# How the split queries of an attention layer reach their stacked layout: 32 small copies from SBUF, or two stores to DRAM and eight loads

## Chip, cores and metric

The kernel runs on one NeuronCore of a Trainium2 chip. The metric is the device time of one execution in microseconds; the figure given is the median of several executions.

## What is computed

Two transformer-like layers over x of shape (8, 512, 128), with AdaLN modulation (a scale, a shift and a gate per batch element). The program handles one batch element (512 tokens) at a time:

```python
# layer 0
h = layernorm(x) * (1 + ca) + sa
x = x + ga * attention(h)          # 8 heads, 2 KV groups, keys and values through a latent of 32, causal softmax
h = layernorm(x) * (1 + cb) + sb
x = x + gb * moe(h)                # 8 experts of 64, top 2, gelu
# layer 1
h = layernorm(x) * (1 + ca) + sa
x = x + ga * selective_scan_mixer(h)   # 256 channels, 16 states, 512 steps
h = layernorm(x) * (1 + cb) + sb
x = x + gb * moe(h)                # 8 experts of 512, top 2, gelu

# the mixer's recurrence, for each of 16 states n
dA  = exp(delta * A[n]);  dBx = (delta * xc) * Bm[n]
h_t = dA_t * h_(t-1) + dBx_t;  y += h_t * Cm[n]
```

The attention's scores need the queries to nearly full f32 precision. Because keys come from a latent of width 32, the key projection is folded into the queries, so that a head's scores are a product over 32 latent rows only. The kernel fills the 128 rows of the array with four such blocks: both queries and keys are split into a high part and a rest, and the four products of the parts are stacked. For the queries the four blocks of rows are high, rest, high, rest (`TERMS = 4`).

## The kernel before, in words

**Engines and order.** Each engine has its own instruction stream written out by hand; semaphores (`signal`, with a target computed per batch) join them. `B = 8` batches are software-pipelined: while batch b goes through the mixer's scan, TensorE and ScalarE do the large experts of batch b-1 in pieces (`SCAN_HIDDEN`, `SCAN_OUTPUT`, `SCAN_GELU` and `SCAN_ADD` say after which step of the scan which piece comes), and the queries, keys and values of batch b+1 are projected in the middle of batch b.

**Queries.** ScalarE copies the projected queries to `q_lat` (two groups g of 128 rows, which are 4 heads j of 32 latent rows, by 512 tokens). VectorE (`split_heads`, L1182) writes the high part `q_hi` and signals `q_split`; GpSimd (`split_rest`, L500) writes the rest `q_lo` and signals `q_rest`. Both lie in the tile `probs`. In `q_terms` all 8 heads must lie on the same 32 partitions, one block of 32 partitions per term. So a head's rows change partitions, and SyncE does this by DMA: `place_queries` (L379 to L390) sends, for each half, group and head, two copies of 32 partitions by 512 floats (64 KB each, 2 KB a partition), 32 in all, each issued at L389. They signal `q_placed`. TensorE's first score product of a batch (`scores(0)`, L717 and L725) waits for all of them, and so does VectorE once in the scan (L1519), since the products that it writes from then on overwrite `probs`.

**The scan.** Before a scan, ScalarE writes the projection `proj` (L1087, signals `pr_out`) and later `dt_log` (L1096, signals `dt_l`). VectorE makes delta (L1499) and u = delta * xc (L1503, once per half c of the channels). SyncE's `spread_rows` (L405 to L418) stores the 16 rows of B to DRAM (L408), waits for that, and loads them back in 8 pairs p, each broadcast to all 128 partitions (L417, 512 KB), into a ring of three slots; pair 1 waits for `dt_l`, and from pair 3 on each waits until GpSimd has used the slot. For each state n and half c, ScalarE computes the decay (L1102) into a ring of three PSUM banks, GpSimd computes the injected term u * B[n] (L455 for state 0, one instruction per half; L457 for the others, both halves at once), VectorE runs the recurrence (`tensor_tensor_scan`, L1514, 32 instructions a batch) and multiplies by C[n], which TensorE has broadcast (L896), into `probs` (L1192); GpSimd (L473, L476) and TensorE (L686) add the 16 products up. After the first three decays ScalarE loads the Gelu table, does four Gelus of the experts of batch b-1 and loads the table for exponentials again (`SCAN_GELU[2]`, L1108, L957, L1111); batch 0 has no experts behind it and no such detour.

**SyncE's order.** SyncE issues the weights, then `place_queries(0)`, then the rows of gates. After that, for each batch b from 0 to 6, `place_queries(b + 1)` and then `spread_rows(b)`, one after the other in one queue; the last batch has `spread_rows(7)` only.

The scan of batch b is called scan b here; there are eight.

## Time and profile before

| | |
|---|---|
| median of 3 runs | 1392.23 us (1390.68 to 1392.95) |
| the profiled execution, its own time | 1388.01 us |
| its span, first to last instruction | 1386.2 us |
| mean granted TensorE clock | 0.942 |
| busy, share of the span: TensorE, VectorE, ScalarE, GpSimd | 82%, 75%, 61%, 38% |
| q_terms<-probs, 256 issues of 64 KB | 2.0 us each from issue to landing |
| probs_T<-b_rows_dram (rows of B), 64 issues of 512 KB | 3.7 us |
| share of 16 DMA engines used by the hardware queue q1 | 13.1% |

The tile `probs_T` shares its space with the scan's tiles (the rows of B, the injected terms and the states), and `step_space` holds delta and u, so the rows of the trace show these names. Row names drop buffer numbers. The engines' names in the rows are PE (TensorE matmul), PEld (its weight load), DVE (VectorE), ACT (ScalarE), POOL (GpSimd) and SP (SyncE); a name with a q is the engine's queue, which issues DMAs.

### The profile page before, as it was taken

The numbers are of one execution on the slowest core, as the hardware profiler recorded it, in microseconds if no ns is written. First come the engines' busy times: TensorE is split into PE (matmuls) and PEld (weight loads), VectorE is DVE, ScalarE is ACT, GpSimd is POOL, SyncE is SP. The second block draws the span as 40 slices with busy tenths as digits, with TensorE's granted clock in tenths as the row PEclk, the third lists the DMA queues.
The fourth block names the chain that finished last, engine by engine and source line by source line (L and its number), as shares of the span: only waits on it lengthen the run. The fifth ranks groups of instructions, "written<-read, shape, count | busy, mean of one in ns | idle before, by whom it ended". The sixth has DMA issues, their size and how long they took to land. (4 is left out here: it accounts for less than half of the span.)

```text
span 1386.2 us, 19199 instructions
## 1 busy us (share of the span) xinstructions
PE 1137.4 (82%) x6304; PEld 727.3 (52%) x6304; DVE 1041.9 (75%) x2396; ACT 847.5 (61%) x1600; POOL 531.9 (38%) x325
## 2 busy tenths in 40 slices
PE   3684678989788887989789887988889897898698
PEld 2551135546555455555656456655556465555456
DVE  2476987589866998579876898669975898669822
ACT  1444346579556866478655876468664785469342
POOL 1003950268102960249202870049402680029400
PEclk8796579999999999999999999999999999999899
DMA  7203200131003200131002300041001300011000
GB/s 262 96 1 108 76 8 1 41 113 31 16 1 105 79 2 15 25 113 46 17 1 62 107 16 17 3 121 61 16 1 43 113 29 9 1 62 62 8 0 9
DMA packets 27731, 65.80 MB, mean 47 GB/s; under 512 B 8048, under 2 KB 8936, under 8 KB 27248
## 3 DMA queue, kind: packets, MB, share of 16 engines
q1 hardware_dynamic: 25328, 56.00, 13.1%
q0 software_dynamic: 1296, 4.20, 1.0%
q10 hardware_dynamic: 1008, 4.38, 0.8%
q8 instruction: 51, 0.84, 0.3%
q14 instruction: 48, 0.39, 0.1%
HBM read 45.40 MB, written 2.38 MB: 34 GB/s over the span
## 5 line engine op out<-in xcount | busy, mean ns | idle before, releaser
L1514 DVE TENSOR_TENSOR_SCAN probs_T<-bank,probs_T 128x512 f32<-128x512 f32 x256 | 303.3, 1210 | 34.6 <-POOL probs_T L455 29.5
L641 PEld LDWEIGHTS bank<-w_w,hidden 128*128 128x128 f32 x2048 | 247.8, 192 | 80.7 <-issue 76.9
L625 PE MATMUL bank<-hT,w_w 128*128 128x512 f32 x512 | 265.6, 636 | 27.2 <-ACT hidden L957 26.3
L457 POOL TENSOR_TENSOR probs_T<-step_space,probs_T 128x1024 f32<-128x1024 f32 x120 | 282.0, 2359 | 1.8 <-DVE probs_T L1514 1.8
L641 PE MATMUL bank<-w_w,hidden 128*128 128x128 f32 x2048 | 251.7, 276 | 9.4 <-DVE expert_sum L1204 9.0
L957 ACT ACTIVATE hidden<-bank,w_b 128x512 f32<-128x512 f32 x256 | 169.6, 686 | 122.2 <-PE bank L625 121.6
L1030 ACT ACTIVATE probs<-bank,row_neg 128x128 f32<-128x128 f32 (+3 forms) x256 | 135.0, 530 | 149.8 <-DVE row_neg L1365 134.7
L1102 ACT ACTIVATE bank<-step_space,a_neg 128x512 f32<-128x512 f32 x256 | 168.6, 684 | 67.8 <-DVE probs_T L1514 49.5
L625 PEld LDWEIGHTS bank<-hT,w_w 128*128 128x128 f32 x512 | 90.9, 198 | 156.1 <-ACT hidden L957 97.9
L1365 DVE TENSOR_REDUCE row_neg<-bank 128x1 f32<-128x128 f32 (+3 forms) x256 | 120.3, 483 | 68.4 <-PE bank L727 66.2
L476 POOL TENSOR_TENSOR step_space<-step_space,probs 128x512 f32<-128x512 f32 x112 | 142.1, 1269 | 61.3 <-DVE probs L1192 61.2
L735 PE MATMUL bank<-w_ident,probs 128*128 128x128 f32 x640 | 117.9, 284 | 48.5 <-ACT probs_T L1006 24.3
L1192 DVE TENSOR_TENSOR probs<-probs_T,bank 128x1024 f32<-128x1024 f32 x128 | 153.1, 1196 | 2.3 <-POOL step_space L473 2.0
L686 PE MATMUL bank<-probs,w_ident 128*128 128x512 f32 x256 | 145.1, 650 | 10.3 <-DVE probs L1192 10.3
L725 PE MATMUL bank<-k_terms,q_terms 128*128 128x128 f32 (+3 forms) x256 | 104.9, 426 | 21.8 <-DMA q_terms<-probs 21.8
L1204 DVE SCALAR_TENSOR_TENSOR expert_sum<-bank,gates,expert_sum 128x128 f32<-128x128 f32 x256 | 71.3, 340 | 56.9 <-PE bank L641 55.3
L482 POOL TENSOR_TENSOR gated_out<-w_out_w,gate 128x256 f32<-128x256 f32 x8 | 5.7, 719 | 270.7 <-DVE xn L1244 270.7
L735 PEld LDWEIGHTS bank<-w_ident,probs 128*128 128x128 f32 x640 | 70.2, 143 | 63.9 <-ACT probs L1030 36.9
L896 PE MATMUL bank<-split,select 96*128 96x512 bf16 x128 | 52.6, 411 | 53.6 <-DVE probs L1192 50.9
L455 POOL TENSOR_TENSOR probs_T<-step_space,probs_T 128x512 f32<-128x512 f32 x16 | 20.3, 1287 | 177.6 <-DMA probs_T<-b_rows_dram 137.3
L1006 ACT ACTIVATE probs_T<-bank 128x128 f32<-128x128 f32 (+3 forms) x176 | 74.8, 425 | 16.0 <-PE bank L735 16.0
L482 POOL TENSOR_TENSOR gated_proj<-w_wprojT,gate 128x512 f32<-128x512 f32 x8 | 17.6, 2203 | 126.8 <-DVE xn L1244 126.8
(186 smaller groups left out, 1682.0 us busy)
## 6 DMA issues: line engine op xcount, KB each, us to landing
probs_T<-b_rows_dram SPq DMA_DIRECT2D x64, 512.0 KB, 3.7
q_terms<-probs SPq DMA_DIRECT2D x256, 64.0 KB, 2.0
w_w<-in_w_dram ACTq DMA_DIRECT2D x2, 2048.0 KB, 13.9
x_in<-in_x_dram POOLq DMA_DIRECT2D x8, 256.0 KB, 3.4
gate<-gate_rows_dram SPq DMA_DIRECT2D x1, 2048.0 KB, 7.2
out_dram<-x_out POOLq DMA_DIRECT2D x7, 256.0 KB, 2.8
step_space<-in_wmod_dram SPq DMA_DIRECT2D x1, 768.0 KB, 5.5
probs_T<-in_wqT_dram SPq DMA_DIRECT2D x1, 512.0 KB, 3.9
```

Of the source, the lines that this page charges most:

```text
L457: ins = nc.gpsimd.tensor_tensor(inject[:, n % 3, :, :], u[:], row.unsqueeze(1).to_broadcast([P, DH, T]), ALU.mult)
L476: ins = nc.gpsimd.tensor_tensor(state_sum[:, 1, :], state_sum[:, 1, :], read[:, n % 2, 1, :], ALU.add)
L625: mm(hid1_bank(n)[:], w["w1"][:, n // C1, n % C1 * P:(n % C1 + 1) * P], hT[3][:], start=True, stop=True).then_inc(hid1_mm.sem, 1)
L641: ins = mm(to[:, t * P:(t + 1) * P], hidden[:, (e * C1 + c) % (2 * C1), t * P:(t + 1) * P], w["w2"][:, e * C1 + c, :], start=(c == 0), sto ...
L686: mm(bank[SUM_BANK][:], ident[:], read[:, n % 2, 0, :], start=(n == 0), stop=(n == NS - 1)).then_inc(sum_mm.sem, 1)
L735: ins = tr(bank[4 + n % 2][:, k * P:(k + 1) * P], probs_ring[:, n % 4, k * P:(k + 1) * P], ident[:])
L957: f(hidden[:, n % (2 * C1), :], hid1_bank(n)[:], ACT.Gelu, bias=w["b1"][:, n:n + 1]).then_inc(hid1_act.sem, 1)
L1030: f(probs_ring[:, n % 4, 0:(i + 1) * P], bank[SCORE_BANK[n % 4]][:, 0:(i + 1) * P], ACT.Exp, bias=row_neg[:, n % 4:n % 4 + 1], accum_out=r ...
L1102: f(decay(k)[:], delta[:, c, :], ACT.Exp, scale=a_neg[:, c, n:n + 1]).then_inc(dec_ok.sem, 1)
L1192: tt(read[:, n % 2, :, :], state[:, n % 2, :, :], bank[C_BANK][:].unsqueeze(1).to_broadcast([P, DH, T]), ALU.mult).then_inc(rd_ok.sem, 1)
L1365: v.reduce_max(row_neg[:, n % 4:n % 4 + 1], bank[SCORE_BANK[n % 4]][:, 0:(i + 1) * P], AX_X, negate=True).then_inc(s_max.sem, 1)
L1514: v.tensor_tensor_scan(state[:, n % 2, c, :], decay(DH * n + c)[:], inject[:, n % 3, c, :], 0.0, ALU.mult, ALU.add).then_inc(st_ok.sem, 1)
```

## The change

The queries' two parts are each stored whole to a DRAM tensor in one transfer of 256 KB (`save_queries`), and each of the four blocks of `q_terms` is then loaded from there in two transfers of 256 KB, one per group, whose source is read in the order row, head, token (`place_queries(b, r)`). For the first batch this happens in one go. For the others the stores stand where the 32 copies stood, and the loads of block r are issued in the scan of the batch before, right behind the rows of B of pair r + 2. VectorE's wait in the scan (L1519) is now for the two stores, TensorE's is for eight loads.

```diff
--- before.py
+++ after.py
@@ -220,6 +220,7 @@
             return bank[DECAY_BANK[k % 3]]
 
 
+        q_dram = nc.dram_tensor("q_parts_dram", (2, P, G * T), F32)
         b_dram = nc.dram_tensor("b_rows_dram", (NS, T), F32)
 
         weights_in, experts_in = sem("weights_in"), sem("experts_in")
@@ -259,7 +260,8 @@
         k_split = signal("k_split", 1)
         q_rest = signal("q_rest", 1)
         k_rest = signal("k_rest", 1)
-        q_placed = signal("q_placed", 16 * TERMS * H)
+        q_saved = signal("q_saved", 32)
+        q_placed = signal("q_placed", 16 * TERMS * G)
         v_mm = signal("v_mm", 1)
         v_out = signal("v_out", 1)
         UNITS = G * NT * HG
@@ -376,18 +378,20 @@
 
         @block.sync
         def _(sp):
-            def place_queries(b):
-
-                for half, source in enumerate((q_hi, q_lo)):
-                    if half == 0:
-                        sp.wait_ge(q_split.sem, q_split.at(b, 1))
-                    else:
-                        sp.wait_ge(q_rest.sem, q_rest.at(b, 1))
-                    for g in range(G):
-                        for j in range(HG):
-                            for r in range(half, TERMS, 2):
-                                sp.dma_start(q_terms[r * L:(r + 1) * L, g * HG + j, :].bitcast(F32), source[j * L:(j + 1) * L, g, :]
-                                             ).then_inc(q_placed.sem, 16)
+            def save_queries(b):
+
+                for half, (signal_of, source) in enumerate(((q_split, q_hi), (q_rest, q_lo))):
+                    sp.wait_ge(signal_of.sem, signal_of.at(b, 1))
+                    sp.dma_start(q_dram[half, :, :], source.rearrange("p g t -> p (g t)")).then_inc(q_saved.sem, 16)
+
+            def place_queries(b, r):
+
+                if r == 0:
+                    sp.wait_ge(q_saved.sem, q_saved.at(b, 32))
+                for g in range(G):
+                    rows = q_dram[r % 2, :, g * T:(g + 1) * T].rearrange("(j l) t -> l j t", l=L)
+                    sp.dma_start(q_terms[r * L:(r + 1) * L, g * HG:(g + 1) * HG, :].bitcast(F32), rows
+                                 ).then_inc(q_placed.sem, 16)
 
             for name in first_a:
                 sp.dma_start(w[name][:], io[name]).then_inc(first_in, 16)
@@ -395,7 +399,9 @@
                 sp.sem_inc(s.sem, 1)
             for name in then:
                 sp.dma_start(w[name][:], io[name]).then_inc(weights_in, 16)
-            place_queries(0)
+            save_queries(0)
+            for r in range(TERMS):
+                place_queries(0, r)
             sp.wait_ge(setup_gate, 4)
             sp.dma_start(gates_dram[:, :], gate_rows[:].rearrange("p k d -> p (k d)")).then_inc(gates_saved, 16)
             sp.wait_ge(gates_saved, 16)
@@ -416,9 +422,11 @@
                         sp.wait_ge(inj_p.sem, inj_p.at(b, 2 * (p - 3) + 3))
                     sp.dma_start(b_wide[:, slot, :, :], rows[:, 2 * p:2 * p + 2, :].to_broadcast([P, 2, T])
                                  ).then_inc(b_rows[p % 3].sem, 16)
+                    if b < B - 1 and 2 <= p < 2 + TERMS:
+                        place_queries(b + 1, p - 2)
 
             for b in range(0, B - 1):
-                place_queries(b + 1)
+                save_queries(b + 1)
                 spread_rows(b)
             spread_rows(B - 1)
 
@@ -714,7 +722,7 @@
                 def scores(n):
                     g, i, j = n // (NT * HG), n // HG % NT, n % HG
                     if n == 0:
-                        pe.wait_ge(q_placed.sem, q_placed.at(b, 16 * TERMS * H))
+                        pe.wait_ge(q_placed.sem, q_placed.at(b, 16 * TERMS * G))
                         pe.wait_ge(k_rest.sem, k_rest.at(b, 1))
                         pe.wait_ge(v_out.sem, v_out.at(b, 1))
                         if ending:
@@ -1516,7 +1524,7 @@
                         if c == 0 and n >= 1:
                             read_product(b, n - 1)
                     if n == 0 and b < B - 1:
-                        dve.wait_ge(q_placed.sem, q_placed.at(b + 1, 16 * TERMS * H))
+                        dve.wait_ge(q_saved.sem, q_saved.at(b + 1, 32))
                     if n in SCAN_ADD:
                         early(EARLY_E + SCAN_ADD.index(n))
                 check()
```

## Rows read from the trace of the kernel before

**Rows 1.** The page, section 1: busy time, share of the span and instructions of each engine.

```profile
PE 1137.4 (82%) x6304; PEld 727.3 (52%) x6304; DVE 1041.9 (75%) x2396; ACT 847.5 (61%) x1600; POOL 531.9 (38%) x325
```

**Rows 2.** Waits, whole run: waiting engine, line, releaser: total us, times, longest.

```profile
POOL probs_T L455 <- DMA probs_T<-b_rows_dram: 137.3, 7, 20.2
...
DVE probs_T L1514 <- POOL probs_T L455: 29.5, 8, 4.9
```

**Rows 3.** Timeline of SyncE: start us, length us, line, operation, count.

```profile
22.20 20.22 SPq L389 DMA_DIRECT2D q_terms<-probs  x32
...
579.96 21.80 SPq L389 DMA_DIRECT2D q_terms<-probs  x32
601.80 0.58 SPq L408 DMA_DIRECT2D b_rows_dram<-proj  x1
```

**Rows 4.** Timeline of all engines around the start of scan 3; idle time before in brackets.

```profile
581.74 2.36 POOL L500 TENSOR_TENSOR probs<-q_lat,probs 128x1024 fp32r<-128x1024 f32 x1
...
594.98 0.69 ACT L1087 ACTIVATE proj<-bank,w_x_proj_b 112x512 f32<-112x512 f32 x1 [0.16 <-PE bank L867]
...
602.47 1.91 ACT L1102 ACTIVATE bank<-step_space,a_neg 128x512 f32<-128x512 f32 x3 [1.96 <-DVE step_space L1499]
...
608.94 2.42 DVE L1514 TENSOR_TENSOR_SCAN probs_T<-bank,probs_T 128x512 f32<-128x512 f32 x2 [4.88 <-POOL probs_T L455]
...
612.07 1.30 ACT L1102 ACTIVATE bank<-step_space,a_neg 128x512 f32<-128x512 f32 x2
```

**Rows 5.** Timeline of ScalarE and VectorE in scan 7.

```profile
1237.21 1.91 ACT L1102 ACTIVATE bank<-step_space,a_neg 128x512 f32<-128x512 f32 x3 [1.96 <-DVE step_space L1499]
...
1246.88 2.67 ACT L1102 ACTIVATE bank<-step_space,a_neg 128x512 f32<-128x512 f32 x4
...
1247.60 2.34 DVE L1514 TENSOR_TENSOR_SCAN probs_T<-bank,probs_T 128x512 f32<-128x512 f32 x2 [2.65 <-ACT bank L1102]
...
1299.42 1.21 DVE L1514 TENSOR_TENSOR_SCAN probs_T<-bank,probs_T 128x512 f32<-128x512 f32 x1
```

**Rows 6.** Timeline: first decays and last scan instruction of scan 1, then scan 6.

```profile
284.93 1.91 ACT L1102 ACTIVATE bank<-step_space,a_neg 128x512 f32<-128x512 f32 x3 [1.96 <-DVE step_space L1499]
...
348.89 1.22 DVE L1514 TENSOR_TENSOR_SCAN probs_T<-bank,probs_T 128x512 f32<-128x512 f32 x1
...
1080.17 1.91 ACT L1102 ACTIVATE bank<-step_space,a_neg 128x512 f32<-128x512 f32 x3 [1.96 <-DVE step_space L1499]
...
1144.61 1.21 DVE L1514 TENSOR_TENSOR_SCAN probs_T<-bank,probs_T 128x512 f32<-128x512 f32 x1
```

**Rows 7.** Timeline of GpSimd and VectorE at the start of scan 0.

```profile
135.07 2.48 POOL L455 TENSOR_TENSOR probs_T<-step_space,probs_T 128x512 f32<-128x512 f32 x2 [18.53 <-DMA probs_T<-b_rows_dram]
...
136.46 2.41 DVE L1514 TENSOR_TENSOR_SCAN probs_T<-bank,probs_T 128x512 f32<-128x512 f32 x2 [2.32 <-POOL probs_T L455]
```

**Rows 8.** Timeline; landing of L389, 22 to 26 us; page; windows (PEclk, DMA share, GB/s last).

```profile
21.07 2.34 POOL L500 TENSOR_TENSOR probs<-q_lat,probs 128x1024 fp32r<-128x1024 f32 x1 [18.89 <-DVE probs L1182]
...
43.96 0.45 PE L725 MATMUL bank<-k_terms,q_terms 128*128 128x128 f32 x1 [21.78 <-DMA q_terms<-probs]
...
DMA to landing us min/median/max: 2.0/2.3/3.3
...
probs_T<-b_rows_dram SPq DMA_DIRECT2D x64, 512.0 KB, 3.7
...
out_dram<-x_out POOLq DMA_DIRECT2D x7, 256.0 KB, 2.8
...
26.00:42.00 16.00, 0.00 (x0) 0.00 (x0) 0.00 (x0) 0.00 (x0) 0.38 (x1) 0.50 0.43 105
...
607.00:609.00 2.00, 2.00 (x3) 0.68 (x2) 0.06 (x1) 0.45 (x1) 1.45 (x2) 0.50 1.01 387
```

**Rows 9.** Timeline of scan 3: a load of rows of B, and GpSimd's first use.

```profile
612.36 0.32 SPq L417 DMA_DIRECT2D probs_T<-b_rows_dram  x1
...
624.00 2.36 POOL L457 TENSOR_TENSOR probs_T<-step_space,probs_T 128x1024 f32<-128x1024 f32 x1
```

## The prediction

> **What bounds the kernel now.** I read the page first: TensorE is busy 82% of the span, no engine all of it [rows 1], so the question is which engine ends each stage. The waits of the whole run came next. Two rows concern the queries' copies. GpSimd's first product of a scan (L455) waited 137.3 us for rows of B from DRAM, seven times, and VectorE's first scan (L1514) waited 29.5 us for that product [rows 2]. There are eight scans, and the one without the DMA wait is the last, the only one with no next queries to place. SyncE's timeline gives the reason [rows 3]. In batch 3 its 32 placements (L389) keep it issuing from 579.96 for 21.80 us, 0.68 us each, and right behind them, at 601.80, comes the store of B (L408). But the projection that this stores was written from 594.98 to 595.67 [rows 4]: the store stood 6.1 us behind placements. At the start the same 32 issues run from 22.20 to 42.42 while TensorE waits 21.78 us for the queries, until 43.96 [rows 3, 8].
>
> Inside a scan VectorE is the engine that ends last; its instructions follow each other without gaps, so what its early part gains moves the end of the stage. Which wait comes next is read from scans 3 and 7, side by side [rows 4, 5].
>
> **The change, part by part.** It removes 32 issues before B, adds 2 stores (256 KB each) there, and 8 loads (256 KB each) behind rows of B. The bytes placed stay 2 MB a batch, plus 0.5 MB stored. The sum has three terms.
>
> *Scans 1 to 6.* SyncE takes the two stores, an issue of 0.58 us each as L408's [rows 3]. In batch 3 the low part that the second waits for is there at 584.10 [rows 4], so SyncE is free some 10 us before the projection is written. So the rows of B come some 6 us earlier and the wait of L455 on the DMA goes. Next late are VectorE's own inputs, then ScalarE. VectorE's idle time there is 4.88 us in scan 3 [rows 4], and this is not what is won: ScalarE, after three decays, leaves for four Gelus and two table loads (SCAN_GELU[2]) and is back at 612.07, 9.60 us after its first decay at 602.47, with nothing of it dependent on B [rows 4]. The decay for the fourth scan instruction cannot be earlier. Scan 7 shows how that looks when B is not late: decay at 1237.21, ScalarE back at 1246.88, the instruction at 1247.60 after 2.65 us idle for ScalarE [rows 5]. So scan 7 is my template. From first decay to last scan instruction it takes 1299.42 - 1237.21 = 62.21 us [rows 5]; scans 1 to 6 take 63.96, 63.49, 64.47, 64.14, 64.12 and 64.44 (the first and the last of the six in [rows 6]). The excesses over 62.21 add up to 11.4 us, which I take; the bounds are nothing (rival 3) and all of VectorE's idle (rival 2).
>
> *Scan 0.* No experts run, so ScalarE has no detour. VectorE idles 2.32 us from 134.14, when the second half of u is made. GpSimd's second product, 1.24 us, then ends near 135.4 instead of 137.55 [rows 7], and the third scan instruction waits for the product after it. Gain 2.1 us.
>
> *The start.* Nothing hides it: TensorE stands still until the queries are placed. The high parts are stored at 22.20 as now; the low ones exist when GpSimd ends at 23.41 [rows 8]. The nearest store of 256 KB (out_dram) lands in 2.8 us [rows 8]; it is on GpSimd's queue, but the low store would land at 23.45 + 2.8 = 26.3. A queue still full of weights costs up to 1.3 us (the first placements landed in 3.3 instead of 2.0 [rows 8]), all of it before the high store, which has that time. Then 8 loads. Issuing them, at 0.58 us, is 4.6 us; what ends last is their transfer. The old placements moved 105 GB/s at a DMA share of 0.43 [rows 8], so a full share onto 32 partitions would be 105 / 0.43 = 244 GB/s, 1.07 us for 256 KB, 8.6 us for eight. With 1.7 us from issue to landing besides the bytes (2.0 less 0.27), the last lands at 26.3 + 1.7 + 8.6 = 36.6: gain 43.96 - 36.6 = 7.4 us. Bounds: at the rate of B's rows onto 128 partitions (387 GB/s over 2 us at full share [rows 8]) each takes 0.68 us and the gain is 10.5; at the old pace, 105 GB/s, each takes 2.5 us and the start loses 4.0. I take 1.07, since same destination, same 2 KB pieces are its nearest row, and as the old pace was set by SyncE's issue, with the engines less than half busy. Whatever follows in batch 0 (gate rows, weights) waits on work that moves with it.
>
> The Trainium skill's page "SBUF — State Buffer", section on the DMA port swizzle, says that 32 partitions reach only half the ports, some 218 GB/s; by that, an estimate, the eight take 9.6 us and the start gains 6.3. Its page "DMA: Bandwidth & Descriptors" (anatomy of one DMA) speaks against a detour over DRAM, since a completion there waits for the slowest receipt, about 2 us; the 2.8 us store in the row already carries that.
>
> *Costed at nothing.* The 8 loads of a scan: behind the rows for pairs 2 to 5 SyncE only waits for GpSimd. In scan 3 the fourth rows were issued at 612.36 and first used at 624.00 [rows 9]; landing takes 3.7 [rows 8], so 7.9 us are spare and two loads take 2.1. If that cover were gone, GpSimd and with it the scan would wait; the rival below prices that. The first three rows of B go ahead of any load. The loads need the stores landed, and those were issued before B. The last pair stands behind rows 5 of 8, with almost half of the 62 us of a scan left before the first user, L725. VectorE's wait at L1519, now for two stores instead of 32 placements, cost no idle time before and none now. Q_terms is free: its last reader was the attention before. TensorE's c_mm waits are for VectorE's products and move with them.
>
> Sum: 7.4 + 2.1 + 11.4 = 20.9 us. The profiled execution took 1388.0 us (span 1386.2), so 1367.1 for it; the median shown is 1392.2, 4.2 us or 0.3% above, and the forecast for a median is 1392.2 - 20.9 = 1371.3.
>
> **Rivals.**
> 1. *The loads at the start keep the old pace* (2.5 us each, DRAM reading no better than 105 GB/s). Start -4.0, scans +13.5: 9.5 us, 1382.7. For: small pieces, few partitions; against: the DMA share of 0.43. Chance 0.10.
> 2. *ScalarE does not hold the scan*, all of VectorE's idle goes: 29.5 less scan 0's 2.3 [rows 2, 7], and less 0.2 that scan 7 waited with B in time, is 27.0 in place of 11.4, total 36.5, 1355.7. Against: scan 7. Chance 0.05.
> 3. *The scans' gain is given back*, TensorE or GpSimd being the one that ends the scan: 7.4 + 2.1 only, 1382.7. Against: scan 7 carries the same expert pieces without a gap. Chance 0.06.
> 4. *SyncE is not freed*, B still waiting behind the low store: only the start counts, 1384.8. The low part was made 11 us before the projection [rows 4]. Chance 0.01.
> 5. *Slower: the loads are slow and hold the queue.* If one takes T us, the start gains 43.96 - 28.0 - 8T, and in seven scans four pairs each stand before rows of B that have 7.9 us to spare. The start alone eats all 13.5 us of the scans at T = 3.7; beyond 3.95 each pair adds 2T - 7.9, 28 times. At T = 4.1 the start loses 16.8 and the pairs 8.4: 11.7 us slower, 1403.9. For it: both kinds share one queue. Against: 64 GB/s would be needed, and the old placements did 105 with the engines half idle. Chance 0.03.
>
> The Trainium skill ("DMA: Bandwidth & Descriptors", queues, rings and completion order) says an engine takes the descriptors of one issuer in order, so rows of B do stand behind loads; by that rival 5's mechanism is real and only its size decides.
>
> **How the numbers follow.** The forecast has 0.73, rivals 0.25, and 0.02 goes to T near 3.7, no change. What a measurement of this kernel can tell from no change is 0.2%, 2.8 us. The forecast's own range is 1365 to 1377: downwards 3.1 for the fast bound of the loads and 3 of the 4.2 us by which the median shown lies above the profiled run; upwards slower loads (T = 1.6) and 1 us from the skew of runs. To keep 8 in 10 with rivals 1 and 3 inside, the high end is 1383. Left out: rivals 2, 4 and 5 and no change, 0.11. Faster by over 0.2%: 0.95; within: 0.02; slower: 0.03.
>
> **What would show it.** In the profile after: L408 right behind L1087 in every batch; L455 waiting for L1503, no more for the DMA; L1514 idle some 2.7 us for L1102 in scans 1 to 6; first decay to last scan instruction about 62.2 us in each; the first L725 near 36.6; eight loads landing in about 3 to 4 us. Wrong would be: L455 or L457 waiting for rows of B in mid-scan, an L725 waiting for q_terms in a later batch, or a first L725 after 44.

## The result, and the profile after

The changed kernel takes 1372.59 us (median of 4 runs, 1369.69 to 1375.60), the kernel before, run beside it, 1391.45 us (4 runs, 1388.37 to 1392.95). The ratio is 0.9867, with a 95% interval from 0.9835 to 0.9899. The medians differ by 18.9 us where 20.9 had been forecast, and the 1372.59 lies 1.3 us above the 1371.3 forecast.

The profiled execution of after took 1374.84 us, with a span of 1373.1 us. Of the four runs it is one of the two long ones (spans 1373.1, 1367.9, 1368.6, 1373.8 us), while the profiled execution of before was the shortest of its own. So the two traces differ by 13.1 us only, and the ledger further down accounts for these 13.1.

The page of after, for [rows 1]: busy times, then from section 5 the scan instructions and from section 6 the issues with their median landing time. Lines stand lower than before, by 8 for most and by 6 for SyncE's in the scan: L414 is the store of B, L423 the load of its rows, L463 and L465 GpSimd's products, L1511 the making of u, L1522 the scan, L1110 the decays, L733 the first product of the attention. L385 is the new store of query parts and L393 their load. Each of these stores moves 512 KB (128 partitions of 4 KB), 1 MB a batch; the section on the change and the prediction call them 256 KB and 0.5 MB.

```profile
PE 1144.8 (83%) x6304; PEld 730.7 (53%) x6304; DVE 1044.7 (76%) x2396; ACT 847.5 (62%) x1600; POOL 535.6 (39%) x325
...
L1522 DVE TENSOR_TENSOR_SCAN probs_T<-bank,probs_T 128x512 f32<-128x512 f32 x256 | 304.4, 1215 | 21.4 <-ACT bank L1110 17.3
...
probs_T<-b_rows_dram SPq DMA_DIRECT2D x64, 512.0 KB, 4.0
q_terms<-q_parts_dram SPq DMA_DIRECT2D x64, 256.0 KB, 6.3
q_parts_dram<-probs SPq DMA_DIRECT2D x16, 512.0 KB, 2.6
```

No engine does less work than before. What changed is whom the engines wait for. Waits of after, whole run, for [rows 2]:

```profile
POOL probs_T L463 <- DVE step_space L1511: 148.3, 16, 39.6
```

GpSimd's wait for rows of B, 137.3 us before, is gone; it waits for u instead. VectorE's 29.5 us for that product shrank to 1.5 us, and its waits for ScalarE's decays grew from 2.6 us, all in scan 7, to 17.3 us in seven scans. Scan 3 shows both. Timeline of after, for [rows 3, 4, 9]:

```profile
590.53 0.69 ACT L1095 ACTIVATE proj<-bank,w_x_proj_b 112x512 f32<-112x512 f32 x1 [0.16 <-PE bank L875]
591.24 0.33 SPq L414 DMA_DIRECT2D b_rows_dram<-proj  x1
...
592.83 4.04 SPq L423 DMA_DIRECT2D probs_T<-b_rows_dram  x3
...
597.45 1.65 POOL L463 TENSOR_TENSOR probs_T<-step_space,probs_T 128x512 f32<-128x512 f32 x1 [14.52 <-DVE step_space L1511]
598.01 1.91 ACT L1110 ACTIVATE bank<-step_space,a_neg 128x512 f32<-128x512 f32 x3 [1.96 <-DVE step_space L1507]
...
603.33 0.34 SPq L423 DMA_DIRECT2D probs_T<-b_rows_dram  x1
...
603.71 0.91 SPq L393 DMA_DIRECT2D q_terms<-q_parts_dram  x2
...
607.64 2.67 ACT L1110 ACTIVATE bank<-step_space,a_neg 128x512 f32<-128x512 f32 x4
...
608.36 2.34 DVE L1522 TENSOR_TENSOR_SCAN probs_T<-bank,probs_T 128x512 f32<-128x512 f32 x2 [2.62 <-ACT bank L1110]
...
616.76 2.35 POOL L465 TENSOR_TENSOR probs_T<-step_space,probs_T 128x1024 f32<-128x1024 f32 x1
```

The store of B stands 0.02 us behind the end of the projection, not 6.1 us behind it. ScalarE leaves after three decays as before and is back 607.64 - 598.01 = 9.63 us after the first (9.60 before), and VectorE waits 2.62 us for it, as it did in scan 7 of before [rows 5]. The load of rows issued at 603.33, with two loads of queries behind it and two ahead, landed after 5.0 us and is first used 13.4 us after its issue.

The start, SyncE's and TensorE's timeline of after, for [rows 8]:

```profile
22.82 1.73 SPq L385 DMA_DIRECT2D q_parts_dram<-probs  x2
...
29.05 3.66 SPq L393 DMA_DIRECT2D q_terms<-q_parts_dram  x8
...
41.40 0.45 PE L733 MATMUL bank<-k_terms,q_terms 128*128 128x128 f32 x1 [17.77 <-DMA q_terms<-q_parts_dram]
```

TensorE begins at 41.40 instead of 43.96: 2.6 us were won where 7.4 had been forecast. This execution's start was a late one: in the five other kernels below with the same start (experiments 2, 3, 7, 8 and 11) TensorE begins at 40.3 to 40.7, and in two with the old start (1 and 9) at 43.9 and 43.4. So the new start is worth some 3 us.

**The ledger of the two traces**, in us. A scan is taken from its first decay to its last scan instruction.

| stretch | before | after | difference | forecast |
|---|---|---|---|---|
| start to first product | 43.96 | 41.40 | -2.56 | -7.4 |
| first product to first decay of scan 0 | 89.50 | 90.36 | +0.86 | 0 |
| scan 0 | 56.19 | 55.05 | -1.14 | -2.1 |
| scans 1 to 6, sum | 384.62 | 372.08 | -12.54 | -11.4 |
| scan 7 | 62.21 | 62.10 | -0.11 | 0 |
| seven stretches between scans, sum | 662.94 | 663.88 | +0.94 | 0 |
| last scan instruction to the end | 86.78 | 88.23 | +1.45 | 0 |
| span | 1386.2 | 1373.1 | -13.1 | -20.9 |

The six scans took 62.17, 62.20, 62.17, 62.18, 61.60 and 61.76 us, against the template's 62.21. The stretches that the change doesn't touch are 3.3 us longer in this execution. The stretches between scans vary by themselves, from 92.6 to 96.1 us each before and from 92.7 to 97.2 after, so a single pair of traces can't decide on them. The last stretch goes with the granted clock: 86.8 us at 0.93 before, 88.2 us at 0.89 after, and with the same instructions 88.6 us at 0.84 in experiment 3 and 87.0 us at 0.93 in experiment 8.

The six scans show what sets their end. In each of scans 1 to 7 of after, the time from the first decay to the last scan instruction is 52.54 us more than the time until ScalarE is back with its fourth decay: 62.17 and 9.63 us in scan 1, 61.60 and 9.06 us in scan 5. Scan 7 of before obeys it too (62.21 and 9.67), while in scans 1 to 6 of before the remainder is 54.0 to 55.4 us.

### The profile page after: what moved, and what is told of

The parts are those of the page before. It is cut to its first block and busy times, and to the rows that moved or that the text cites. A ratio compares the mean times of both kernels' runs of the same rounds, so it can differ in the third digit from the quotient of the medians.

```text
span 1373.1 us, 19023 instructions
## 1 busy us (share of the span) xinstructions
PE 1144.8 (83%) x6304; PEld 730.7 (53%) x6304; DVE 1044.7 (76%) x2396; ACT 847.5 (62%) x1600; POOL 535.6 (39%) x325
## 3 DMA queue, kind: packets, MB, share of 16 engines
HBM read 62.17 MB, written 10.76 MB: 53 GB/s over the span
## 5 line engine op out<-in xcount | busy, mean ns | idle before, releaser
L1522 DVE TENSOR_TENSOR_SCAN probs_T<-bank,probs_T 128x512 f32<-128x512 f32 x256 | 304.4, 1215 | 21.4 <-ACT bank L1110 17.3
L633 PE MATMUL bank<-hT,w_w 128*128 128x512 f32 x512 | 267.7, 640 | 27.2 <-ACT hidden L965 26.3
L465 POOL TENSOR_TENSOR probs_T<-step_space,probs_T 128x1024 f32<-128x1024 f32 x120 | 282.4, 2359 | 11.2 <-DVE probs_T L1522 11.2
L1110 ACT ACTIVATE bank<-step_space,a_neg 128x512 f32<-128x512 f32 x256 | 167.8, 683 | 54.9 <-DVE probs_T L1522 36.7
L633 PEld LDWEIGHTS bank<-hT,w_w 128*128 128x128 f32 x512 | 91.6, 199 | 156.4 <-ACT hidden L965 97.7
L733 PE MATMUL bank<-k_terms,q_terms 128*128 128x128 f32 (+3 forms) x256 | 107.2, 433 | 17.8 <-DMA q_terms<-q_parts_dram 17.8
L463 POOL TENSOR_TENSOR probs_T<-step_space,probs_T 128x512 f32<-128x512 f32 x16 | 23.3, 1458 | 148.3 <-DVE step_space L1511 148.3
## 6 DMA issues: line engine op xcount, KB each, us to landing
w_w<-in_w_dram ACTq DMA_DIRECT2D x2, 2048.0 KB, 14.1
```

Of the source, the lines that this page charges most:

```text
L465: ins = nc.gpsimd.tensor_tensor(inject[:, n % 3, :, :], u[:], row.unsqueeze(1).to_broadcast([P, DH, T]), ALU.mult)
L633: mm(hid1_bank(n)[:], w["w1"][:, n // C1, n % C1 * P:(n % C1 + 1) * P], hT[3][:], start=True, stop=True).then_inc(hid1_mm.sem, 1)
L1110: f(decay(k)[:], delta[:, c, :], ACT.Exp, scale=a_neg[:, c, n:n + 1]).then_inc(dec_ok.sem, 1)
L1522: v.tensor_tensor_scan(state[:, n % 2, c, :], decay(DH * n + c)[:], inject[:, n % 3, c, :], 0.0, ALU.mult, ALU.add).then_inc(st_ok.sem, 1)
```

## The experiments

**1. The new scans with the old start.** Batch 0 is placed by the 32 copies again, the later batches as in the changed kernel.

```diff
-            save_queries(0)
-            for r in range(TERMS):
-                place_queries(0, r)
+            place_direct(0)
```

> The changed kernel, but the queries of batch 0 are placed as before, by 32 copies; the other seven batches keep the detour over DRAM. Theory (most of the gain is in the scans, where rows of B are no longer behind 32 issues): only the 2.6 us go that the first score product came earlier (41.4 instead of 44.0), so about 1372.6 + 2.6 = 1375.2 against 1391.4, a gain of 16 us; scans 1 to 6 still take 61.6 to 62.2 us from first decay to last scan instruction. Rival (the start is worth the 7.4 us that the prediction gave it, and a late reading hides it): about 1380.

Measured: 1374.01 us (6 runs, 1367.39 to 1381.23), ratio 0.9894 [0.9870, 0.9919]. TensorE's first product is back at 43.86, and scans 1 to 6 take 60.5 to 62.2 us: 14.1 us by the medians, and by the ratios four fifths of the change's gain, without the new start. Scan 4 is the shortest, 60.53 us with ScalarE back after 7.99 us, again 52.54 us apart. Windows of the first 8 us of scan 3 of the changed kernel, and of this scan 4 (granted clock is the third number from the end):

```profile
598.01:606.01 8.00, 5.67 (x20) 2.90 (x19) 7.45 (x13) 5.52 (x8) 7.37 (x5) 0.79 0.77 216
```

```profile
756.25:764.25 8.00, 5.67 (x31) 3.49 (x30) 7.46 (x13) 7.13 (x10) 7.37 (x5) 1.00 0.84 218
```

In both TensorE stands idle for 2.3 us, waiting for ScalarE's first Gelu. In the changed kernel its granted clock is then 0.50 (1.2 GHz) from 602 to 605, and ScalarE waits 1.58 and 0.86 us for its products before the last two Gelus; here the clock stays at 1.00 (2.4 GHz), and the two waits are 0.64 and 0.17 us. So 1.6 us of ScalarE's usual absence of 9.6 us go with TensorE's lower clock. Scan 5 of experiment 5 is the same: clock 1.00, ScalarE back after 7.99 us, 60.53 us.

**2. The new start with the old scans.** The kernel before, with batch 0 alone sent over DRAM.

```diff
-            place_queries(0)
+            save_queries(0)
+            for r in range(TERMS):
+                place_saved(0, r)
```

> The kernel before, but the queries of batch 0 alone go over DRAM in two stores and eight loads. Theory: the first score product near 41.4 instead of 44.0, all scans as before (63.5 to 64.5 us, first scan instruction idle 4 to 5 us for GpSimd's first product), total 1391.4 - 2.6 = 1388.8, within what can be told from no change. Rival (the start carries 7 us): 1384.

Measured: 1385.73 us (median of 12 runs, one of which took 6003.51 us and is left out of the ratio), ratio 0.9974 [0.9962, 0.9986]. Its waits, and then its timeline at the start:

```profile
POOL probs_T L474 <- DMA probs_T<-b_rows_dram: 135.6, 7, 20.2
...
DVE probs_T L1533 <- POOL probs_T L474: 27.7, 8, 4.9
```

```profile
40.66 0.44 PE L744 MATMUL bank<-k_terms,q_terms 128*128 128x128 f32 x1 [17.97 <-DMA q_terms<-q_parts_dram]
```

The scans wait as in [rows 2], and the start gains 43.96 - 40.66 = 3.3 us, the whole time 2.4 (1388.11 to 1385.73). The two parts add up within their intervals: 1.06% and 0.26% are 1.32%, and both together gave 1.33%.

**3. The loads ahead of B.** All eight loads stand right behind the stores, so SyncE's queue holds 2 MB of them shortly before B, but it issues only 10 transfers instead of 32.

```diff
                 save_queries(b + 1)
+                for r in range(TERMS):
+                    place_queries(b + 1, r)
...
-                    if b < B - 1 and 2 <= p < 2 + TERMS:
-                        place_queries(b + 1, p - 2)
```

> The changed kernel, but all eight loads of the next batch are issued right behind the two stores, ahead of the store of B, and none in the scan. Theory A (what held the rows of B was SyncE's time to issue, 20 us; eight issues of 0.45 us end well before the projection is written): B is stored on time, its first rows land up to 2 to 3 us later because the loads, 1.3 to 1.5 us each, still fill the DMA engines, and ScalarE's detour, for which VectorE idles 2.6 us anyway, hides most of that: the time stays at 1372.6, plus at most 5 us. Theory B (the place behind the rows of B is what wins, since transfers in the queue hold B as much as issues did): the rows come 6 us late again and the time goes back to about 1385 or more.

Measured: 1372.00 us (4 runs, 1370.27 to 1373.06), ratio 0.9876 [0.9861, 0.9892], the changed kernel's within the intervals. Its scan 3:

```profile
579.69 3.66 SPq L393 DMA_DIRECT2D q_terms<-q_parts_dram  x8
588.65 0.31 SPq L414 DMA_DIRECT2D b_rows_dram<-proj  x1
...
598.69 2.42 DVE L1522 TENSOR_TENSOR_SCAN probs_T<-bank,probs_T 128x512 f32<-128x512 f32 x2 [1.67 <-POOL probs_T L463]
...
605.82 2.34 DVE L1522 TENSOR_TENSOR_SCAN probs_T<-bank,probs_T 128x512 f32<-128x512 f32 x2 [1.29 <-ACT bank L1110]
```

Eight issues take 3.66 us, where 32 took 21.80, and the store of B is issued as soon as its projection exists. GpSimd's first product waits for rows of B again, and VectorE 1.67 us for that product, but it then waits 1.29 us for ScalarE instead of 2.62: ScalarE sets the same end. The scans take 62.18 to 62.23 us. So what the scans win is SyncE's issue time; the place behind rows of B adds nothing to the time, as ScalarE's absence covers the queue's delay.

**4. The start without DRAM, on two queues.** The 32 copies of batch 0 are shared: the high parts by SyncE, the low ones by ScalarE's queue.

```diff
-            save_queries(0)
-            for r in range(TERMS):
-                place_queries(0, r)
+            place_direct(sp, 0, q_hi, q_split)
...
+            place_direct(act, 1, q_lo, q_rest)
             iteration(0, False, True)
```

> The changed kernel, but batch 0 is placed directly, without DRAM, the 16 copies of the high part issued by SyncE and the 16 of the low part by ScalarE's queue, which is idle then. Theory (the direct copies were bound by one engine's issue at 0.63 us each, with the DMA engines 43% busy): 16 issues take 10 us side by side, the first score product comes near 36 instead of 41.4, total 1372.6 - 5.4 = 1367. Rival (the issue of a copy is bound by something both queues share): 32 issues still take 20 us, first product near 44, total 1375.

Measured: 1367.84 us (4 runs, 1365.17 to 1370.26), ratio 0.9847 [0.9830, 0.9865]. Timeline of its start:

```profile
21.88 10.14 SPq L385 DMA_DIRECT2D q_terms<-probs  x16
...
23.94 10.36 ACTq L385 DMA_DIRECT2D q_terms<-probs  x16
...
35.85 0.44 PE L740 MATMUL bank<-k_terms,q_terms 128*128 128x128 f32 x1 [12.79 <-DMA q_terms<-probs]
```

The old copies had been held by their issue: each queue spends 0.63 to 0.65 us on one, and two queues side by side send the 32 in 12.4 us instead of 20.2. TensorE begins 5.6 us before the changed kernel's (4.5 to 4.8 before the other traces with its start), and the median is 4.8 us lower, though the intervals of the two ratios overlap. By the traces, the detour over DRAM is not the best start for this kernel.

**5. The high parts first.** The start over DRAM, but the four loads of high parts go out when the high store has landed, and the low ones behind.

```diff
+            sp.wait_ge(hi_saved, 16)
+            for r in (0, 2):
+                place_queries(0, r, first=True)
+            sp.wait_ge(q_saved.sem, q_saved.at(0, 32))
+            for r in (1, 3):
+                place_queries(0, r)
```

> The changed kernel, but in batch 0 the four loads of the high part are issued as soon as the high store has landed, and only the other four wait for the low store. The changed kernel started its eight loads at 29.0, 4.5 us after the low store was issued, and had the first score product at 41.4. Theory (store and loads are a chain, each with its landing time, and the loads then run at 1.3 us each): four loads run while the low store lands; the first score product comes 1.5 to 3 us earlier, near 39, the total 2 us earlier, 1370 to 1371. Rival (the DMA engines are full from 23 us on, so that order changes nothing): 41.4 and 1372.6.

Measured: 1366.76 us (4 runs, 1365.64 to 1369.46), ratio 0.9855 [0.9832, 0.9879]. Its timeline, and its windows (stretch, length, busy time of PE, PEld, DVE, ACT and POOL, granted clock, DMA share, GB/s):

```profile
26.68 3.66 SPq L394 DMA_DIRECT2D q_terms<-q_parts_dram  x8
...
38.80 0.44 PE L742 MATMUL bank<-k_terms,q_terms 128*128 128x128 f32 x1 [15.38 <-DMA q_terms<-q_parts_dram]
```

```profile
28.00:32.00 4.00, 0.00 (x0) 0.00 (x0) 0.00 (x0) 0.00 (x0) 0.00 (x0) 0.54 1.02 232
32.00:36.00 4.00, 0.00 (x0) 0.00 (x0) 0.00 (x0) 0.00 (x0) 0.00 (x0) 0.50 1.06 209
```

The loads go out 2.4 us earlier than in the changed kernel's trace and the product comes 2.6 us earlier. Half of that is not the edit: the high store landed at 26.67 and the low one at 27.91, so 1.2 us of waiting were saved, and against the other traces with the changed kernel's start the product comes 1.5 to 1.9 us earlier. The loads themselves take 38.80 - 26.68 = 12.1 us, with the DMA engines full. Against the changed kernel the whole time lies inside both intervals.

**6. The same bytes onto all partitions.** Eight loads of 256 KB whose destination is 128 partitions, not 32. The stacked queries of batch 0 thus hold other rows than they should, so this kernel is for its start alone.

```diff
-            for r in range(TERMS):
-                place_queries(0, r)
+            for h in range(H):
+                sp.dma_start(q_terms[:, h, :].bitcast(F32), q_dram[h % 2, :, h // HG * T:(h // HG + 1) * T]
+                             ).then_inc(q_placed.sem, 16)
```

> Measures what bounds the eight loads of batch 0. They move the same number of bytes from the same DRAM tensor in the same pieces of 2 KB, but each goes onto 128 partitions of one head instead of 32 partitions of four heads, so batch 0's stacked queries hold the wrong rows and its output differs. Theory (32 partitions are what slows them, 1.3 us for 256 KB where rows of B onto 128 partitions took 0.7): eight loads take 5 to 6 us, the first score product comes near 36 to 37. Rival (reading 2 KB pieces from DRAM bounds them): still near 41.4.

Measured (one run, 1369.26 us). Timeline, and one window of it:

```profile
28.01 3.66 SPq L405 DMA_DIRECT2D q_terms<-q_parts_dram  x8
...
37.78 0.44 PE L735 MATMUL bank<-k_terms,q_terms 128*128 128x128 f32 x1 [14.28 <-DMA q_terms<-q_parts_dram]
```

```profile
32.00:36.00 4.00, 0.00 (x0) 0.00 (x0) 0.00 (x0) 0.00 (x0) 0.00 (x0) 0.50 0.91 333
```

From first issue to product it takes 9.8 us; the changed kernel takes 41.40 - 29.05 = 12.35. With the DMA engines full or nearly so, 128 partitions take 333 GB/s, where 32 took 232 and 209 in experiment 5: the few partitions cost 2.6 us here. The 36 to 37 that the theory gave were not reached; the engines were not full before 32 us (shares 0.48 from 28 to 30 and 0.76 from 30 to 32).

**7. Heavier traffic behind each pair.** Eight more transfers of 256 KB each, DRAM to DRAM, behind every pair of loads, to see whether rows of B do stand behind them (rival 5).

```diff
                         place_queries(b + 1, p - 2)
+                        for k in range(8):
+                            sp.dma_start(x_dram[(b * TERMS + p - 2) * 8 + k, :, :], q_dram[k % 2, :, 0:T]).then_inc(more, 16)
```

> The changed kernel with eight further transfers of 256 KB, DRAM to DRAM, behind each pair of loads in the scan (data nobody reads). It tests the slower rival of the prediction, that loads in the queue hold rows of B. In the changed kernel rows 3 are issued at 603.3 and used at 616.8, 9 us more than they need to land. Theory (transfers of one queue are served in turn): 10 transfers at 1.3 us are 13 us per pair, some 4 us over the cover and then more for each further pair; GpSimd (L465) waits for rows of B in the middle of each of the first seven scans, 15 to 25 us a scan, total 1480 to 1550. Rival (the DMA engines take them beside each other and B is not held): no such wait, 1373 to 1380.

Measured (one run): 1419.92 us. Its waits and landing time:

```profile
POOL probs_T L469 <- DMA probs_T<-b_rows_dram: 76.8, 20, 5.9
...
DVE probs_T L1526 <- POOL probs_T L469: 38.2, 16, 4.7
```

```profile
probs_T<-b_rows_dram SPq DMA_DIRECT2D x64, 512.0 KB, 10.8
```

Rows of B land in 10.8 us instead of 4.0, GpSimd waits for them 20 times in mid-scan and VectorE for GpSimd. The mechanism is real. Its price is smaller than was expected: scans 1 to 6 are 4.6 to 8.6 us longer than in the changed kernel, 6.3 on average, and scan 0 is 10.5 us longer.

With the two loads of the change alone nobody waits, but the delay is there. The median of 4.0 us takes in the rows that stand ahead of all loads or far behind them; those of pairs 3 to 5, behind them, landed in 4.4 to 6.9 us in scans 1 to 6 (3.3 to 5.3 before) and much later in scan 0. Its three loads of rows between 137 and 148 us (L423), from issue to landing:

```profile
DMA to landing us min/median/max: 8.7/10.0/10.2
```

The same three took 3.3 to 3.7 us in the kernel before. The one issued at 137.06 had 2.9 us to spare before its first use, where the kernel before had 8.3. From 137 to 150 us the DMA engines were full at only 153 GB/s; in experiments 5 and 8 the same rows landed in 4.5 to 5.1 us. Why they were slower here stays open.

**8. ScalarE's absence in two halves.** To see what stands behind ScalarE, its detour (four pieces of Gelu) is split into two of two pieces, in the changed kernel. It needs three planned tables of the scan to be moved by a place.

```diff
-SCAN_GELU = {2: (12, 16), 7: (16, 18), ...
+SCAN_GELU = {2: (12, 14), 4: (14, 16), 7: (16, 18), ...
```

> The changed kernel, but ScalarE's first detour in a scan is cut in two: Gelus 12 and 13 after decay 2, Gelus 14 and 15 after decay 4 (one more pair of table loads), and TensorE's pieces that need them (first product 16, outputs 12 to 15) move one or two states later. Theory (ScalarE's detour is what holds VectorE now): VectorE's idle time for ScalarE before the fourth scan instruction, 2.6 us, goes; part comes back at a later decay, since detours now lie closer; I work out 1.5 us less per scan, first decay to last scan instruction 60.7 instead of 62.2, seven scans, total about 1372.6 - 10 = 1362. Rival (TensorE has no room for the moved pieces, rival 3 of the prediction in another place): idle time of VectorE for TensorE or for expert outputs appears, the interval stays at 62 or grows, total 1372 or more.

Measured: 1372.72 us (4 runs, 1371.20 to 1374.52), ratio 0.9871 [0.9852, 0.9890]: no change. Two of the scan instructions of its scan 3, and its windows of the 12 us behind that scan and of the whole stretch up to the next:

```profile
610.03 2.34 DVE L1522 TENSOR_TENSOR_SCAN probs_T<-bank,probs_T 128x512 f32<-128x512 f32 x2 [0.63 <-ACT bank L1110]
...
615.84 1.22 DVE L1522 TENSOR_TENSOR_SCAN probs_T<-bank,probs_T 128x512 f32<-128x512 f32 x1 [1.22 <-ACT bank L1110]
```

```profile
659.83:671.83 12.00, 8.79 (x48) 6.90 (x48) 9.90 (x22) 4.21 (x20) 3.35 (x3) 0.86 0.07 20
...
659.83:755.34 95.51, 82.25 (x530) 56.03 (x531) 69.85 (x228) 54.34 (x135) 13.74 (x11) 0.98 0.07 25
```

Windows of the changed kernel for the same stretches:

```profile
660.18:672.18 12.00, 8.60 (x56) 6.31 (x56) 11.36 (x25) 5.30 (x23) 3.34 (x3) 1.00 0.07 20
...
660.18:754.97 94.79, 82.45 (x530) 55.24 (x531) 70.00 (x228) 54.35 (x135) 13.72 (x11) 0.98 0.08 26
```

ScalarE does hold the scan: with its first absence shorter, back after 5.8 us, scans 1 to 7 take 61.52 us instead of about 62.2. But the wait of 2.6 us doesn't vanish. It comes back as 0.63 and 1.22 us, so 0.65 a scan is all that is won, and the stretches behind the scans take 95.5 us instead of 94.8, so the period of a batch stays at 157.0 us. A spell of low granted clock now falls on the first 12 us behind the scan, where TensorE gets 48 matmuls done instead of 56. That spell goes with the loss, and it does so in the changed kernel's own trace: behind scan 5 the first 12 us have a clock of 0.86 too, and that stretch takes 95.6 us, where the four before it, at 1.00, take 94.0 to 94.9. That it causes the loss was not shown, nor why it moves. The 157.0 us are no floor: scan 4 of experiment 1 and the stretch behind it take 155.3.

**9. The same split in the kernel before**, to see what it does while B is late.

> The same cut of the detour in the kernel before. Theory (there the rows of B hold the scan first, and ScalarE's detour lies beside that wait): the first scan instruction still waits 4 to 5 us for GpSimd; in scans 1 to 6 the fourth was held by VectorE itself, so nothing is won there, only in scan 7; intervals of 63.5 to 64.5 stay within 0.5 us, total within 3 us of the kernel before. Rival (the detour holds the scan in both kernels): 10 us less here too, 1378.

Measured: 1394.87 us (10 runs, 1391.83 to 1399.93), ratio 1.0039 [1.0019, 1.0059], 4.9 us slower. Two scan instructions of its scan 3:

```profile
615.89 2.41 DVE L1514 TENSOR_TENSOR_SCAN probs_T<-bank,probs_T 128x512 f32<-128x512 f32 x2 [4.38 <-POOL probs_T L455]
...
639.01 1.22 DVE L1514 TENSOR_TENSOR_SCAN probs_T<-bank,probs_T 128x512 f32<-128x512 f32 x1 [0.54 <-ACT bank L1102]
```

The first scan instruction still waits for rows of B, so ScalarE's earlier return is worth nothing there; and scans 1 to 6 take 64.9 to 66.4 us instead of 63.5 to 64.5, more than the 0.5 us that the theory allowed. Scan 7, where B is on time, takes 61.51 us, as in experiment 8. So where B is late, ScalarE's first absence lies beside the wait for it and doesn't set the end; that it is the second absence which costs these 0.7 to 2.0 us is argued, not shown.

**10. Both: the start on two queues and the split.**

> The changed kernel with both edits: batch 0 placed directly by two queues, and the detour cut in two. If the two act in different places their gains add: 1367.8 - 10 = about 1358. If the detour's cut gains nothing: 1368.

Measured: 1367.10 us (4 runs, 1362.87 to 1368.22), ratio 0.9825 [0.9804, 0.9846]. Scans of 61.51 us and 95.5 us between them: the median is 0.7 us below that of the two-queue start alone (0.9847), and the intervals overlap. The split adds nothing that can be told.

**11. GpSimd held back in scan 0**, so that its products no longer run beside VectorE's making of u.

```diff
-                    pool.wait_ge(u_ok.sem, u_ok.at(b, c + 1))
+                    pool.wait_ge(u_ok.sem, u_ok.at(b, DH if b == 0 else c + 1))
```

> The changed kernel, but in batch 0 GpSimd's first product waits for both halves of u. It asks why scan 0 won 1.1 us and not 2.1: in the changed kernel VectorE's second product for u (L1511) took 1.63 us instead of 0.69 and ran beside GpSimd's first product, which took 1.65 instead of 1.26. Theory (two such instructions side by side slow each other): apart, they take 0.69 and 1.26 again; the first scan instruction then comes at the end of the first half's product, about 0.3 us later than now, so nothing is won in all. Rival (the 0.94 us has another cause, such as VectorE waiting for something the record does not show): L1511 still takes 1.6.

This kernel's one execution took 2204.61 us: TensorE's 128x512 products of the experts (L633) took 1144 ns on average, where in the repeat below they take 640 ns. So it says nothing on the edit.

> The changed kernel, but in batch 0 GpSimd's first product waits for both halves of u; the same edit as in the run before, repeated because that execution ran all of TensorE's products at half speed. VectorE's second product for u at 0.69 us instead of 1.63, GpSimd's two products at 1.26 each, the first scan instruction some 0.3 us later than in the changed kernel; total 1372 to 1376. Rival: L1511 still takes 1.6 us.

Measured (one run): 1372.19 us. The start of its scan 0, and then that of the changed kernel:

```profile
128.17 0.69 DVE L1511 TENSOR_TENSOR step_space<-step_space,xc 128x512 f32<-128x512 f32 x1
...
128.94 2.48 POOL L463 TENSOR_TENSOR probs_T<-step_space,probs_T 128x512 f32<-128x512 f32 x2 [16.02 <-DVE step_space L1511]
...
130.34 2.41 DVE L1522 TENSOR_TENSOR_SCAN probs_T<-bank,probs_T 128x512 f32<-128x512 f32 x2 [1.48 <-POOL probs_T L463]
```

```profile
131.04 0.68 DVE L1507 SCALAR_TENSOR_TENSOR step_space<-step_space,probs_T 128x512 f32<-128x512 f32 x1
...
131.20 1.65 POOL L463 TENSOR_TENSOR probs_T<-step_space,probs_T 128x512 f32<-128x512 f32 x1 [16.49 <-DVE step_space L1511]
...
131.76 1.63 DVE L1511 TENSOR_TENSOR step_space<-step_space,xc 128x512 f32<-128x512 f32 x1
...
133.47 1.26 POOL L463 TENSOR_TENSOR probs_T<-step_space,probs_T 128x512 f32<-128x512 f32 x1 [0.63 <-DVE step_space L1511]
...
137.16 1.22 DVE L1522 TENSOR_TENSOR_SCAN probs_T<-bank,probs_T 128x512 f32<-128x512 f32 x1 [1.11 <-POOL probs_T L465]
```

VectorE's product, begun under GpSimd's, takes 1.63 us instead of 0.69. GpSimd's takes 1.65 instead of 1.26, and it began under the VectorE instruction before (L1507, until 131.72); in scan 3 it takes 1.65 us as well, with L1507 beside its start and L1511 beginning only 0.17 us before its end. Apart, both have their old durations, but GpSimd's first product begins 1.3 us later against the first decay, and the scan takes 55.36 us where it took 55.05. Nothing is won either way.

## Why the prediction was right, and where its terms were off

The forecast held: faster, 18.9 us of 20.9 between the medians. That the two are so close is partly luck. The three terms measure 16.2 us in the two traces, and the interval of the ratio leaves 14 to 23 us; the start fell short by far more than the scans' term exceeded.

**Scans 1 to 6: right, by the mechanism given.** SyncE was free when the projection came, the wait on rows of B went, and the next one late was ScalarE coming back from its Gelus, so that every scan fell to scan 7's 62.2 us. The term was 11.4 us and measured 12.5; two scans came out at 61.6 and 61.8 because ScalarE was back after 9.06 and 9.22 us, not 9.63. Experiments 1 and 2 give the split between scans and start. The constant 52.54 us between ScalarE's return and a scan's length, over returns from 7.99 to 9.67 us, and experiment 8 show that ScalarE held the scan; experiment 9 shows that it did not while B was late. The weights were off: of the sum, the scans were given two thirds and bring four fifths.

**Scan 0: half the size.** The term said that GpSimd's two first products, 1.24 us each, would follow on the earlier rows, 2.1 us won. It took each duration as it was. What it left out is that the first product, no longer late, lies beside VectorE's making of the second half of u and stretches it from 0.69 to 1.63 us. The second product waits for that, and the third scan instruction for the product behind it: 5.40 us after the first decay (137.16 - 131.76), against 6.52 before. 1.1 us were won.

**The start: mis-sized, 2.6 us instead of 7.4.** The step had three parts, and each was off.
- The low parts were made 0.8 us later in this execution: GpSimd's product of them ended at 24.20 instead of 23.41. In experiment 2 it was 0.3 us later only (23.73), and the gain there was 3.3 us: this part of the shortfall is mostly this execution's own.
- The low store was priced at 2.8 us, by an output store of 256 KB. The page lists the stores at 512 KB, twice what the prediction said (1 MB a batch, not 0.5), and here they queue behind the last weights, one of them of 512 KB too, and the low store behind the high one: the DMA engines were full from 26 to 28 us (422 GB/s at a share of 1.03), and the stores landed at 27.80 and 29.03. The loads could go out at 29.05, 4.8 us behind the low part: 2.0 us more than priced. In the later batches the same store lands in 2.6 us, so the price of the row held for an empty queue.
- The eight loads were priced at 10.3 us from 244 GB/s, scaled up from 105 GB/s at a share of 0.43. They took 12.35 us, 2.05 more: they landed 1.28 us apart instead of 1.07, which is 1.5 us over seven, and the first one 3.3 us after its issue, where 2.8 had been given. This window of the changed kernel shows full engines at less:

```profile
31.00:39.00 8.00, 0.00 (x0) 0.00 (x0) 0.00 (x0) 0.00 (x0) 0.00 (x0) 0.50 1.06 211
```

Scaling a rate by the busy share overrated it: 244 GB/s against 211. The Trainium skill's page "SBUF — State Buffer", section on the DMA port swizzle, gives some 218 GB/s for 32 partitions: the trace agrees (211 GB/s). The estimate of 6.3 us by that page was nearer to the measured gain, though not near, since it took the store as priced.

0.8 + 2.0 + 2.05 = 4.8 us, the difference between 7.4 and 2.6.

**The rivals.** Rival 1, the loads at the old pace: no; 211 GB/s, and the old pace was SyncE's issue (experiment 4). Rival 2, all of VectorE's idle goes: no; in its place the waits for ScalarE rose from 2.6 to 17.3 us. Rival 3, the scans' gain given back: not in the change, but this is what befell the 0.65 us a scan of experiment 8. Rival 4, SyncE not freed: no. Rival 5, loads hold the queue: its mechanism was shown by experiment 7. In the change it never decided, but the cover was thinner than the 7.9 us that the prediction costed at nothing: it fell to 2.9 us in scan 0. Of the prediction's signs, two did not come: the first L725 (now L733) stood at 41.40 and not near 36.6, and the eight loads of a batch landed in 6.3 us (median), not in 3 to 4.

**What stays open**: why the stretches between scans grow by what experiment 8 wins in the scans, and why rows of B landed so late in scan 0.

The best start tried is not the changed kernel's. On two queues without DRAM the kernel takes 1367.84 us (0.9847), with high parts first 1366.76 (0.9855); their intervals overlap with each other and with that of the change, but TensorE begins 5.6 and 2.6 us earlier in their traces, 4.5 and 1.5 us of it at least against every other trace with the changed start.

## What to carry to other kernels

Many small transfers on one queue cost their issue time even when all of them are hidden, since a late and urgent one stands behind them: count issues between an urgent transfer and its data, and fuse or move those that aren't urgent. Where an early wait goes, look for an instance of the same stage that never had it and take its length, not the idle time, as what remains. A detour over DRAM is priced with its own bytes and with what the queue carries at that time, against the same copies issued from a second queue.

## What the runs showed of the hardware

- VectorE and GpSimd each slowed when an operation on two operands in SBUF began under the other's: 0.69 to 1.63 us and 1.26 to 1.65 us for 128x512 (experiment 11). In the changed kernel VectorE's begins at 131.76 under GpSimd's, which ends at 132.85, and ends at 133.39, 0.54 us behind it; in scan 3 it begins 0.17 us before GpSimd's end and ends 0.56 us behind it. It looks as if it had waited for GpSimd's end. The Trainium skill's page "SBUF — State Buffer", section "SBUF: two separate sides", describes the port pair that the two engines share as a lock that the first holds for its whole instruction; the row fits that.
- With full DMA engines (share 1.0), loads from DRAM in 2 KB pieces ran at 209 to 232 GB/s onto 32 partitions; onto 128 they ran at 333 GB/s at a share of 0.91 (experiments 5 and 6).
- A queue issued copies of 64 KB from 32 partitions at 0.63 to 0.68 us each, and loads of 256 KB at 0.46 us (3.66 us for eight); a second engine's queue issued at the same pace beside the first (experiment 4).
- A store of 512 KB landed in 4.9 us behind the weights and in 2.6 us (median) in all, the later batches' among them.
- After TensorE had stood idle for 2.3 us in a scan, its granted clock fell to 0.50 (1.2 GHz) for some 3 us in scan 3 of the changed kernel and stayed at 1.00 (2.4 GHz) in scan 4 of experiment 1; ScalarE, which waits for its products, was back 1.6 us earlier there.
- One execution (2204.61 us, experiment 11) had TensorE products of 1144 ns instead of 640 from end to end, while its granted clock was given as 1.00.
